# An attention kernel on one core: which engine's queue issues the two guard-row transfers of each unit

## The chip, the cores and the metric

The kernel runs on one core of a Trainium2 chip. Its time is the device time of one execution in microseconds, compared as the median of several runs. Lower is better.

## The reference, cut to what matters

The input x has 2048 rows of 128 numbers. The first block is full attention over all 2048 rows with 16 heads of 8 numbers and an additive bias; six further layers of windowed attention and feed-forward follow, which this change doesn't touch. The first block:

```
x = x + attn(layernorm(x))
q, k, v = (x @ Wq.T + bq), (x @ Wk.T + bk), (x @ Wv.T + bv)      # 16 heads of 8
logits = li[:, :, None, :] + lj[:, None, :, :] + rel_b           # 3 relations per (i, j)
relation_probs = softmax(logits, axis=-1)
bias = einsum('bijk,hk->bhij', relation_probs, logical_bias)
attn_scores = q·k / scale + gate * bias
out = softmax(attn_scores, axis=-1) @ v ;  out @ Wo.T + bo
```

## The kernel before, in words

The function `attention` computes the first block. The 2048 queries are 16 blocks of 128, and each block has two halves of 8 heads. One half of one block is a *unit*: there are 32 units, four to a `body` (`ul` 0 to 3), eight bodies (`it` 0 to 7). A unit has 16 *steps*, one for each block of 128 keys (`jb`), so the attention has 512 steps.

Each step makes two score tiles on TensorE. Tile **b** belongs to the present unit: query-key products (L529), then the relation bias (L537). ScalarE takes its exponential into `prob` (L660), and one step later TensorE multiplies `prob` with the values (L571). Tile **a** is the same product 24 steps ahead, and only its maximum over the keys is kept (L811, VectorE). The softmax needs that maximum. When a unit's 16 tiles a are through, VectorE and TensorE reduce them to one number for each head and query (events `max0`, `max1` after steps 8 and 10 of the unit before), split its negative into three bf16 parts, and transpose these (event `guard` after step 12; VectorE copies the result to `guardT` in step 13, L868). These 24 rows of 128 are the *guard rows*. Two small transfers, each 12 rows of 256 bytes, carry them from `guardT` into rows 48 to 50 of `qst` (L995). With them the product of tile b has 51 rows in place of 48, and so already subtracts the maximum. In step 0 of a unit TensorE first issues the query-key products of tile a, and then waits for `guard_dma` before those of tile b. There is no double buffer of `guardT`.

The relation bias comes from a second pipeline. Eight steps are a *window*: ScalarE, GpSimd and VectorE compute a quarter (512 keys) of the relation probabilities of a block in `stage`. SyncE sends it to DRAM (`quarter_out`, L973, waits for `lo_done`), waits until it has landed, and issues eight transfers of 128 KB back into `pst` in another layout (`quarter_in`, L986). Each unit has two windows and so two such bursts. The function `moved` issues one window's transfers.

The order on each engine is written out by hand: there is no scheduler. An engine's queue is in order, so whatever stands behind a wait waits too. SyncE's order in a unit is: at a block's start the queries of the next block (L963), `moved` for the even window, at a block's start the store of the finished block (L1026), `moved` for the odd window, `guards`.

In the last body no relation probabilities are left to compute after its first two windows, so `moved` issues nothing there after its first unit.

Of the kernel before, what the change touches and what calls it, by code (L numbers as in the profile page):

```python
# [27 lines left out]
NB = S // P  # L28
H, HD = 16, 8
HH = H // 2  # L30
# [3 lines left out]
GUARD_ROW = len(TERMS) * HD  # L34
# [354 lines left out]
def attention(nc, io, keep):  # L389

    with ExitStack() as ctx:
        sb = lambda n, s, d=F32: ctx.enter_context(nc.sbuf_tensor(n, s, d))
        sem = lambda n: ctx.enter_context(nc.semaphore(n))
        kst, qst, v9, coef = keep["kst"], keep["qst"], keep["v9"], keep["coef"]
# [32 lines left out]
        m_read = sem("m_read")  # L428
# [45 lines left out]
        def events_before(it, ul, step, first, last):  # L474

            n = 3 if first else 20 * it
            for w in range(ul + 1):
                e = unit_events(w, first, last)
                n = n + sum(1 for k in e if w < ul or k < step)
            return n  # L480
# [172 lines left out]
        @block.scalar  # L653
        def _(act):
            def exp_tile(b, st, first):
                act.wait_ge(b_done, b + 1)
                if not (first and st < 2):

                    act.wait_ge(pv_done, b - 1)
                act.activation(prob[:, st % 2, :], psS[:, slot_of("b", st)].rearrange("p a b -> p (a b)"), ACT.Exp)\  # L660
                   .then_inc(e_done, 1)

            def clamp(n, q, r, par):

                act.wait_ge(own_done, n // 4 + 1)
                if not (isinstance(n, int) and n < 2):
                    act.wait_ge(x_first, n - 1) if early(n - 2) else act.wait_ge(x_done, n - 1 - FIRST)
                    act.wait_ge(e2_done, n - 1)
                act.activation(top[:, r], f[:, 1, quarter(q)], ACT.Relu, bias=own[:, par, 1:2]).then_inc(u_done, 1)

            def third(n, r):

                act.wait_ge(top_done, n + 1)
                if not (isinstance(n, int) and n < 2):
                    act.wait_ge(pm_done, n - 1)
                act.activation(rec[:, r], top[:, r], ACT.Exp, scale=-1.0).then_inc(e2_done, 1)

            def pair_exp(n, r, par):

                act.wait_ge(x_first, n + 1) if early(n) else act.wait_ge(x_done, n + 1 - FIRST)  # L680
                act.activation(rel[:, r, 0], rel[:, r, 0], ACT.Exp, bias=own[:, par, 0:1])
                act.activation(rel[:, r, 1], rel[:, r, 1], ACT.Exp, bias=own[:, par, 1:2]).then_inc(re_done, 1)

            def first_part(n, r):

                act.wait_ge(pm_done, n + 1)
                if not (isinstance(n, int) and n < 2):
                    act.wait_ge(p_dma[r], n // 2 * (16 * PO))
                act.activation(stage[:, r, :, 0, :], rel[:, r], ACT.Copy).then_inc(hi_done, 1)

            def body(it, first=False, last=False):
                for st in range(4 * NB):
                    k, o, n, q, r, opens, closes = windows(it, st, last)
                    par = (k + EARLY) // 4 % 2
                    exp_tile(it * (4 * NB) + st, st, first)
                    if opens and o == 0:
                        clamp(n, q, r, par)
                    if closes and o == 2:
                        first_part(n - 1, 1 - r)
                    if opens and o == 2:  # L700
                        third(n, r)
                    if opens and o == 3:
                        pair_exp(n, r, par)

            for n in range(EARLY):
                clamp(n, n % 4, n % 2, n // 4)
                third(n, n % 2)
                pair_exp(n, n % 2, n // 4)
                if n >= 1:
                    first_part(n - 1, (n - 1) % 2)  # L710
            body(0, first=True)
            for it in range(1, 7):
                body(it)
            body(7, last=True)
# [241 lines left out]
        @block.sync  # L956
        def _(sp):
            def queries(block_no, par):
                t0 = block_no * P
                for hp in range(2):  # L960
                    src = io["q_stack"].rearrange("r (pair hp) s -> hp r pair s", hp=2)[hp]
                    src = src[:, :, t0:t0 + P] if isinstance(t0, int) else src[:, :, bass.ds(t0, P)]
                    sp.dma_start(qst[64 * hp:64 * hp + GUARD_ROW, par], src).then_inc(q_dma[par], 16)  # L963

            def quarter_out(n, q, r, blk, par):

                sp.wait_ge(lo_done, n + 1)
                take_waits(sp, sp_waits)
                if not (isinstance(blk, int) and blk < 2):
                    sp.wait_ge(pst_dma[par][q], blk // 2 * (16 * PI))  # L970
                take_waits(sp, sp_waits)
                there = p_parts[par, :, :, :, quarter(q)].rearrange("k a c j -> c (k a) j")
                sp.dma_start(there, stage[:, r].rearrange("p k a j -> p (k a) j")).then_inc(p_dma[r], 16)  # L973

            def quarter_in(n, q, r, blk, par):

                sp.wait_ge(p_dma[r], n // 2 * (16 * PO) + 16 * PO)
                take_waits(sp, sp_waits)
                if not (isinstance(blk, int) and blk < 2):
                    sp.wait_ge(b_done, (blk - 2) * (2 * NB) + NB + 4 * q + 4)  # L980
                take_waits(sp, sp_waits)
                for k in range(2):
                    for t in range(4):
                        w = 64 * k + G * t
                        there = p_parts[par, k, t // 3, :, quarter(q)].rearrange("(g i) j -> i g j", i=G)
                        sp.dma_start(pst[w:w + G, par, :, quarter(q)], there).then_inc(pst_dma[par][q], 16)  # L986

            def guards(read, ul):

                sp.wait_ge(m_read, read)  # L990
                par, half = (ul // 2) % 2, ul % 2
                for hp in range(2):
                    r = 64 * hp + GUARD_ROW
                    dst = qst[r:r + 3, par, HH // 2 * half:HH // 2 * (half + 1), :]
                    sp.dma_start(dst, guardT[12 * hp:12 * (hp + 1), :]).then_inc(guard_dma, 16)  # L995

            def moved(it, k, last):

                if not (last and k > 1):
                    n = it * 8 + k + EARLY - 1  # L1000
                    m = k + EARLY - 1
                    quarter_out(n, m % 4, m % 2, it * 2 + m // 4, m // 4 % 2)
                    quarter_in(n, m % 4, m % 2, it * 2 + m // 4, m // 4 % 2)

            def body(it, first=False, last=False):
                for ul in range(4):
                    blk = it * 2 + ul // 2
                    if ul % 2 == 0 and not (first and ul == 0) and not (last and ul == 2):

                        sp.wait_ge(b_done, blk * (2 * NB))  # L1010
                        take_waits(sp, sp_waits)
                        queries(blk + 1, (ul // 2 + 1) % 2)
                    moved(it, 2 * ul, last)
                    if ul % 2 == 0 and not (first and ul == 0):
                        store(blk - 1, events_before(it, ul, 6, first, last) + 1)
                    moved(it, 2 * ul + 1, last)
                    if not (last and ul == 3):
                        guards(events_before(it, ul, 12, first, last) + 1, (ul + 1) % 4)

            def store(blk, read):  # L1020

                sp.wait_ge(m_read, read)
                take_waits(sp, sp_waits)
                dst = io["x1"].rearrange("(b p) d -> p b d", p=P)
                dst = dst[:, blk, :] if isinstance(blk, int) else dst[:, bass.ds(blk, 1), :].rearrange("p a d -> p (a d)")
                sp.dma_start(dst, x1[:]).then_inc(x1_dma, 16)  # L1026

            queries(0, 0)
            queries(1, 1)
            for n in range(EARLY - 1):  # L1030
                quarter_out(n, n % 4, n % 2, n // 4, n // 4)
                quarter_in(n, n % 4, n % 2, n // 4, n // 4)
            guards(3, 0)
            body(0, first=True)
            for it in range(1, 7):
                body(it)
            body(7, last=True)
            store(NB - 1, 20 * 7 + 20 - 3 + 3)
            sp.wait_ge(x1_dma, 16 * NB)
# [747 lines left out]
```

## Time and profile before

| | |
|---|---|
| median of 3 runs | 3796.5 us (3795.06 to 3797.84) |
| the profiled execution | 3794.38 us, its span 3792.6 us |
| PE busy | 3167.1 us (84%) |
| DVE busy | 2489.9 us (66%) |
| ACT busy | 2070.3 us (55%) |
| POOL busy | 2294.9 us (61%) |
| DMA queue q1 (SyncE's) | 276232 packets, 252.24 MB, 31.3% of 16 engines' span |
| DMA queue q10 (ScalarE's) | 720 packets, 0.20 MB, 0.0% |

PE is TensorE, PEld its weight loads, DVE VectorE, ACT ScalarE, POOL GpSimd. SPq and ACTq rows are DMA issues of SyncE and ScalarE. An issue is not counted as busy time, and its row shows how long the issuing queue was taken, not how long the transfer took. "[5.32 <-DMA qst<-guardT]" behind a row says that the engine sat idle for 5.32 us before it, and that the transfer named ended this. The attention steps run from about 184 to 1604 us of the span; the first 184 us prepare, and the local layers fill the rest.

### The profile page before, as it was taken

To read this page: it belongs to the slowest core of one execution; us is meant where nothing else is said; L and a number is where in the kernel's file an instruction comes from. 1 tells how busy PE (TensorE), PEld (TensorE's weight loads), DVE (VectorE), ACT (ScalarE), POOL (GpSimd) and SP (SyncE) were. 2 spreads that over 40 slices of the span, in tenths; PEclk is the share of its full clock that TensorE was granted. 3 is DMA by queue.
4 is the path that set the end of the run, shared out by engine and by line. 5 is a ranking of instruction groups with operands and counts; after the bars stand their busy time and mean duration, and the time that the engine had idled before them with its cause. 6 is when DMAs were issued, how large, how long until landed. Compare 5 with 4: busy or idle time off the path is not lost. (4 is left out here: it accounts for less than half of the span.)

```text
span 3792.6 us, 121537 instructions
## 1 busy us (share of the span) xinstructions
PE 3167.1 (84%) x52983; PEld 2322.6 (61%) x52983; DVE 2489.9 (66%) x3404; ACT 2070.3 (55%) x2481; POOL 2294.9 (61%) x1606
## 2 busy tenths in 40 slices
PE   3488888888888888858888888888888888888885
PEld 2366666676666666636666666666666666666664
DVE  4766666766766666346666766766766667667663
ACT  2255445554544454426666666666666666666663
POOL 1544444444444443067777777777777777777773
PEclk7699999999999999979999999999999999999997
DMA  4544444444443443042223222322232232222221
GB/s 106 101 72 78 74 76 77 75 72 78 80 75 73 72 73 72 14 131 62 52 53 76 71 56 59 86 58 56 53 93 54 53 79 69 54 61 52 59 56 37
DMA packets 277483, 260.21 MB, mean 69 GB/s; under 512 B 106264, under 2 KB 220841, under 8 KB 276825
## 3 DMA queue, kind: packets, MB, share of 16 engines
q1 hardware_dynamic: 276232, 252.24, 31.3%
q8 instruction: 418, 6.85, 0.8%
q14 instruction: 113, 0.92, 0.1%
q10 hardware_dynamic: 720, 0.20, 0.0%
HBM read 98.30 MB, written 40.37 MB: 37 GB/s over the span
## 5 line engine op out<-in xcount | busy, mean ns | idle before, releaser
L660 ACT ACTIVATE prob<-psS 128x1024 f32<-128x1024 f32 x512 | 524.2, 1024 | 729.6 <-PE psS L537 726.2
L811 DVE TENSOR_TENSOR colmax<-psS,colmax 128x1024 f32<-128x1024 f32 x480 | 587.5, 1224 | 455.6 <-PE psS L537 453.4
L537 PE MATMUL psS<-diag,pst 128*128 128x64 bf16 x16384 | 609.6, 198 | 8.0 <-issue 7.8
L529 PE MATMUL psS<-qst,kst 48*128 48x128 bf16 (+1 forms) x8192 | 387.3, 225 | 250.1 <-DMA qst<-guardT 139.1
L537 PEld LDWEIGHTS psS<-diag,pst 128*128 128x128 f16 x16384 | 543.0, 101 | 69.0 <-issue 19.0
L1265 PE MATMUL R<-wqkv,xsT 128*128 128x512 f32 x1152 | 554.9, 605 | 1.5 <-ACT qT L1401 1.1
L745 POOL TENSOR_TENSOR rel<-rel,rec 128x1024 f32<-128x1024 f32 x64 | 151.9, 2373 | 626.6 <-DVE rec L824 626.6
L529 PEld LDWEIGHTS psS<-qst,kst 48*128 48x128 bf16 (+1 forms) x8192 | 242.0, 97 | 407.4 <-issue 163.0
L1529 POOL TENSOR_TENSOR pr<-pr,rnq 128x1024 f32<-128x1024 f32 x96 | 182.7, 1903 | 397.1 <-DVE pr L1610 397.1
L571 PE MATMUL psO<-prob,v 128*9 128x128 f32 x8192 | 333.1, 281 | 2.7 <-issue 2.1
L1265 PEld LDWEIGHTS R<-wqkv,xsT 128*128 128x128 f32 x1152 | 197.7, 191 | 162.2 <-issue 160.6
L1486 POOL TENSOR_TENSOR rnq<-ssq,half 128x16 f32<-128x16 f32 x96 | 281.6, 2934 | 8.0
L1486 POOL TENSOR_TENSOR rnk<-ssq,half 128x16 f32<-128x16 f32 x96 | 281.2, 2929 | 8.0
L1332 PE MATMUL R<-w,xnT 128*128 128x341 f32 x384 | 179.2, 601 | 100.7 <-DVE xnT L1594 100.7
L1499 POOL TENSOR_TENSOR t<-t 128x1024 f32<-128x1024 f32 x96 | 227.1, 2366 | 33.1 <-DVE t L1550 33.1
L1556 DVE TENSOR_REDUCE ssq<-sq 128x16 f32<-128x1024 f32 x192 | 233.2, 1214 | 11.2 <-ACT sq L1419 3.7
L1547 DVE TENSOR_TENSOR t<-R,tab 128x1024 f32<-128x1024 f32 x192 | 228.4, 1190 | 15.8 <-PE R L1265 9.3
L824 DVE RECIPROCAL rec<-tot 128x128 f32<-128x128 f32 x256 | 238.3, 937 | 0.0
L1603 DVE TENSOR_TENSOR gs<-hs 128x341 f32<-128x341 f32 x96 | 49.6, 516 | 285.9 <-ACT hs L1450 285.9
L1436 ACT ACTIVATE kT<-R 64x1024 f32<-64x1024 f32 x192 | 195.4, 1018 | 68.6 <-PE R L1316 67.4
L1520 POOL TENSOR_TENSOR t<-t 128x1024 f32<-128x1024 f32 x96 | 225.6, 2350 | 10.8 <-DVE t L1550 10.8
L1401 ACT ACTIVATE prT<-R 128x1024 f32<-128x1024 f32 x96 | 98.2, 1023 | 224.1 <-PE R L1286 224.1
(190 smaller groups left out, 6327.9 us busy)
## 6 DMA issues: line engine op xcount, KB each, us to landing
v<-vs SPq DMA_DIRECT2D x576, 128.0 KB, 2.4
pst<-p_parts SPq DMA_DIRECT2D x512, 128.0 KB, 4.9
p_parts<-stage SPq DMA_DIRECT2D x64, 512.0 KB, 3.1
v<-vs SPq DMA_DIRECT2D x384, 64.0 KB, 2.0
wqkv<-in_L_ffn_Wqkv SPq DMA_DIRECT2D x18, 512.0 KB
q_stack<-qpart SPq DMA_DIRECT2D x6, 512.0 KB
qst<-q_stack SPq DMA_DIRECT2D x32, 96.0 KB, 4.4
wo<-in_L_ffn_Wo SPq DMA_DIRECT2D x6, 512.0 KB
```

Source lines behind the costliest of these rows:

```text
L529: pe.matmul(dst[:, hp, P * p:P * (p + 1)], kst[r, pair, P * jb:P * (jb + 1)], qst[r, par, pair, :], start=(p == 0), stop=False, skip_group ...
L537: last = pe.matmul(o, pst[:, par, g, P * jb:P * (jb + 1)], diag[:, par, g, h0:h0 + HH // 2, :], start=False, stop=(g == NG - 1), skip_grou ...
L571: last = pe.matmul(psO[32 * c:32 * c + HD + 1, P * s:P * (s + 1)], v9[:, jb, HH * half + hl, :], prob[:, jb % 2, col:col + P], start=(jb = ...
L660: act.activation(prob[:, st % 2, :], psS[:, slot_of("b", st)].rearrange("p a b -> p (a b)"), ACT.Exp)\
L811: dve.tensor_tensor(dst, src, dst, ALU.max).then_inc(a_read, 1)
L824: dve.reciprocal(rec[:, r, cols], tot[:, r, cols]).then_inc(rr_done, 1)
L1265: last = pe.matmul(R[bank][:, c, :], xsT[:, par, :], w[:, INNER * which + 512 * c:INNER * which + 512 * (c + 1)], start=True, stop=True)
L1486: pool.tensor_tensor(dst, ssq[:, i, :], half1[:, 0:LH], ALU.pow).then_inc(m["rn_done"], 1)
L1499: pool.tensor_tensor(t1[:, 1, :], t1[:, 1, :], t2[:, 1, :], ALU.add).then_inc(m["add_done"], 1)
L1520: pool.tensor_tensor(t1[:, 0, :], t1[:, 0, :], t2[:, 0, :], ALU.add).then_inc(m["q_added"], 1)
L1547: dve.tensor_tensor(o1, q, tb(2 * i, 0, LD), ALU.mult)
L1556: dve.tensor_reduce(ssq[:, i, :], sq[:].rearrange("p (h d) -> p h d", d=LD), AX.X, ALU.add)\
```

## The change

ScalarE issues the guard transfers in place of SyncE. The function moves over unchanged but for the engine, and with its wait (`m_read`, that VectorE has written `guardT`). ScalarE calls it in step 13 of each unit but the last, directly behind the exponential of step 13, and once ahead of the first body.

```
@@ block.scalar
+            def guards(read, ul):
+                act.wait_ge(m_read, read)
+                par, half = (ul // 2) % 2, ul % 2
+                for hp in range(2):
+                    r = 64 * hp + GUARD_ROW
+                    dst = qst[r:r + 3, par, HH // 2 * half:HH // 2 * (half + 1), :]
+                    act.dma_start(dst, guardT[12 * hp:12 * (hp + 1), :]).then_inc(guard_dma, 16)
...
                     exp_tile(it * (4 * NB) + st, st, first)
+                    ul, jb = divmod(st, NB)
+                    if jb == 13 and not (last and ul == 3):
+                        guards(events_before(it, ul, 12, first, last) + 1, (ul + 1) % 4)
...
+            guards(3, 0)
             body(0, first=True)
@@ block.sync
-            def guards(read, ul):
-                sp.wait_ge(m_read, read)
...
                     moved(it, 2 * ul + 1, last)
-                    if not (last and ul == 3):
-                        guards(events_before(it, ul, 12, first, last) + 1, (ul + 1) % 4)
...
-            guards(3, 0)
             body(0, first=True)
```

SyncE's order over two units of the middle of the attention, before. L973 and L986 are `quarter_out` and `quarter_in`, L1026 stores a finished block, L963 loads the next block's queries:

```order
L1026 DMA x<-x_sb 128x128
L973 DMA p_parts<-stage 128x4x512
L986 DMA pst<-p_parts 16x8x512 x8
L995 DMA qst<-guardT 3x4x128 x2
L973 DMA p_parts<-stage 128x4x512
L986 DMA pst<-p_parts 16x8x512 x8
L973 DMA p_parts<-stage 128x4x512
L986 DMA pst<-p_parts 16x8x512 x8
L995 DMA qst<-guardT 3x4x128 x2
L963 DMA qst<-q_stack 48x8x128 x2
```

The same place of SyncE after the change (L986 and L999 are now `quarter_out` and `quarter_in`, L1028 the store, L976 the queries):

```order
L1028 DMA x<-x_sb 128x128
L986 DMA p_parts<-stage 128x4x512
L999 DMA pst<-p_parts 16x8x512 x8
L986 DMA p_parts<-stage 128x4x512
L999 DMA pst<-p_parts 16x8x512 x8
L986 DMA p_parts<-stage 128x4x512
L999 DMA pst<-p_parts 16x8x512 x8
L976 DMA qst<-q_stack 48x8x128 x2
```

The guard transfers stood behind the eight `pst` transfers of the odd window; they are gone from this queue, and nothing else changed its place.

ScalarE's order over the second half of a unit and the start of the next, before. L660 is the exponential of a step; the others belong to the relation windows:

```order
L681 ACTIVATE rel<-rel,own 128x512
L682 ACTIVATE rel<-rel,own 128x512
L660 ACTIVATE prob<-psS 128x1024 x5
L669 ACTIVATE top<-f,own 128x512
L660 ACTIVATE prob<-psS 128x1024 x2
```

And after:

```order
L681 ACTIVATE rel<-rel,own 128x512
L682 ACTIVATE rel<-rel,own 128x512
L660 ACTIVATE prob<-psS 128x1024 x2
L698 DMA qst<-guardT 3x4x128 x2
L660 ACTIVATE prob<-psS 128x1024 x3
L669 ACTIVATE top<-f,own 128x512
L660 ACTIVATE prob<-psS 128x1024 x2
```

The two issues stand between the exponentials of steps 13 and 14; those of steps 14, 15 and of step 0 of the next unit are queued behind them.

## Rows read from the trace of the kernel before

**Rows 1.** The page: one of the costliest groups, busy time, then idle time ahead
```profile
L529 PE MATMUL psS<-qst,kst 48*128 48x128 bf16 (+1 forms) x8192 | 387.3, 225 | 250.1 <-DMA qst<-guardT 139.1
```

**Rows 2.** TensorE's waits, 200 to 1600: who for whom, us, times, longest
```profile
PE psS L529 <- DMA qst<-guardT: 134.0, 29, 6.1
PE psS L537 <- issue: 7.8, 10, 1.4
PE psS L529 <- issue: 4.1, 6, 1.1
PE psO L571 <- issue: 2.1, 3, 0.8
```

**Rows 3.** Timeline, steps 13 of a unit to 1 of the next: start, length
```profile
856.37 1.03 ACT L660 ACTIVATE prob<-psS 128x1024 f32<-128x1024 f32 x1 [1.95 <-PE psS L537]
856.78 5.10 SPq L986 DMA_DIRECT2D pst<-p_parts  x8
857.04 0.27 DVE L868 CAST guardT<-psM 24x128 bf16<-24x128 f32 x1
858.66 1.02 ACT L660 ACTIVATE prob<-psS 128x1024 f32<-128x1024 f32 x1 [1.26 <-PE psS L537]
859.81 1.11 PE L537 MATMUL psS<-diag,pst 128*128 128x64 bf16 x32
860.84 0.62 PE L571 MATMUL psO<-prob,v 128*9 128x128 f32 x16
861.40 0.40 PE L529 MATMUL psS<-qst,kst 48*128 48x128 bf16 x8
861.93 1.55 SPq L995 DMA_DIRECT2D qst<-guardT  x2
867.12 0.60 PE L529 MATMUL psS<-qst,kst 51*128 51x128 bf16 x8 [5.32 <-DMA qst<-guardT]
867.65 1.89 PE L537 MATMUL psS<-diag,pst 128*128 128x64 bf16 x32
870.38 0.62 PE L529 MATMUL psS<-qst,kst 48*128 48x128 bf16 x16
```

**Rows 4.** Windows: busy us of each engine, PEclk, DMA share, GB/s
```profile
864.00:865.00 1.00, 0.00 (x0) 0.00 (x0) 0.00 (x0) 0.00 (x0) 0.00 (x0) 1.00 1.14 122
866.00:867.00 1.00, 0.00 (x0) 0.00 (x0) 0.00 (x0) 0.00 (x0) 0.00 (x0) 0.92 0.05 8
867.00:869.00 2.00, 1.88 (x34) 1.69 (x35) 0.27 (x1) 0.00 (x0) 0.00 (x0) 0.50 0.03 8
1508.00:1604.00 96.00, 93.08 (x2483) 70.62 (x2478) 37.00 (x56) 48.42 (x48) 0.00 (x0) 1.00 0.02 4
```

**Rows 5.** Timeline of the last body, one unit's end, where no `pst` burst runs
```profile
1539.96 0.27 DVE L868 CAST guardT<-psM 24x128 bf16<-24x128 f32 x1
1540.26 1.44 SPq L995 DMA_DIRECT2D qst<-guardT  x2
1544.32 0.85 PE L529 MATMUL psS<-qst,kst 48*128 48x128 bf16 x16
1546.70 0.76 PE L529 MATMUL psS<-qst,kst 48*128 48x128 bf16 x16
```

**Rows 6.** ScalarE's timeline: step 0 of units 0, 29 and 30
```profile
184.48 1.02 ACT L660 ACTIVATE prob<-psS 128x1024 f32<-128x1024 f32 x1 [25.69 <-PE psS L537]
1507.28 1.02 ACT L660 ACTIVATE prob<-psS 128x1024 f32<-128x1024 f32 x1 [7.44 <-PE psS L537]
1546.25 1.02 ACT L660 ACTIVATE prob<-psS 128x1024 f32<-128x1024 f32 x1 [1.36 <-PE psS L537]
```

**Rows 7.** DMA issues by line: ns min/median/max; ScalarE's own at the start
```profile
L995 SPq DMA_DIRECT2D qst<-guardT x64: 698/736/806, 179.3 to 1573.6; - x64
L231 ACTq DMA_DIRECT2D bk<-in_L_attn_bk x1: 453/453/453, 2.6 to 2.6; - x1
```

**Rows 8.** TensorE's timeline beside an even window's burst
```profile
388.45 1.08 PE L537 MATMUL psS<-diag,pst 128*128 128x64 bf16 x31 [1.36 <-issue]
```

More of the change, by code:

```diff
@@ L986, in quarter_in @@
                         sp.dma_start(pst[w:w + G, par, :, quarter(q)], there).then_inc(pst_dma[par][q], 16)
-            def guards(read, ul):
-                sp.wait_ge(m_read, read)
[L991 to L995, printed above, removed]
             def moved(it, k, last):
```

## The prediction

> **What bounds the kernel now.** I read the page first. In the attention part TensorE is busy in nearly every slice, and the group of the query-key products is the one group of TensorE with much idle time: 250.1 us, of which 139.1 us ended with the arrival of `qst<-guardT` [rows 1]. The list of waits, cut to the attention's steps, says how that is spread: 29 times, 134.0 us, 6.1 us the longest [rows 2], so 4.62 us each. The thirtieth wait of the page, ahead of the first unit, makes up the other 5.1 us. No other wait of TensorE there reaches 16 us in sum. So TensorE sets the pace of the attention, and once in each unit it stands still for the guard rows.
>
> The timeline says why [rows 3]. VectorE has the guard rows ready at 857.31 us (857.04 + 0.27). SyncE is then already issuing the eight `pst` transfers of the odd window, from 856.78 for 5.10 us, and gets to the guard rows at 861.93, 4.6 us after they were ready. TensorE had issued tile a's products of step 0 at 861.40 and wanted tile b's at 861.80. It gets them at 867.12. Of that time the guard transfers spend about 3.5 us behind the burst: the 16 DMA engines are still full at 864 to 865 (share 1.14), and empty at 866 to 867 (0.05) [rows 4].
>
> The pause has a second price. After it the granted clock is 0.50, the 1.2 GHz level, at 867 to 869, where TensorE worked throughout [rows 4]; the relation products of that step take 1.89 us and not 1.11 [rows 3]. From the products of tile a in step 0 to those of step 1 it takes 870.38 - 861.40 = 8.98 us, where the same distance without a wait is 1546.70 - 1544.32 = 2.38 us [rows 3, 5]. The difference, 6.60 us, is 5.32 us of idle time and 1.28 us of slow clock.
>
> The trace contains the changed order too, as far as SyncE can show it. In the last body the odd window of units 29 and 30 has no burst, so nothing stands in front of the guard issue. In unit 29 the rows are ready at 1540.23, are issued at 1540.26, and TensorE goes through all 16 products of step 0 at 1544.32 with no wait [rows 5]. The lead is 1544.72 - 1540.26 = 4.46 us, and it was enough on idle DMA engines.
>
> **The change part by part.** *The wait goes.* Two ways to size it:
> - From the parts: 134.0 us of idle time [rows 2], and 29 times 1.28 us of slow clock = 37 us. Together 171 us. It is a lower end: in some units the slow clock lasts longer than in the one shown.
> - From whole units: units 0 to 28 take (1507.28 - 184.48) / 29 = 45.61 us each, and unit 29, whose end has no wait, 1546.25 - 1507.28 = 38.97 us [rows 6]. The difference, 6.64 us, times 29 is 193 us. It is an upper end: unit 29 also lacks the instruction stalls below, and as a block's second unit the two small products of a finished block.
>
> I take the middle, 182 us. The clock's part goes with the pause: from 1508 to 1604, with two unit ends without a wait, the granted clock is 1.00 over the whole 96 us with TensorE busy for 93.08 [rows 4].
>
> *What ScalarE takes on.* Two issues in each of 31 units, and two ahead of the first. On SyncE the same issue takes 0.736 us, on ScalarE the only ones there are took 0.453 us [rows 7], so 0.9 to 1.5 us for the pair. ScalarE ends the exponential of step 13 at 857.40, and the one of step 14 starts at 858.66: a gap of 1.26 us [rows 3]. The wait on `m_read` costs nothing, since the rows are ready at 857.31, before that exponential ends. With the longer pair (857.40 to 858.9) the exponential of step 14 ends at 859.9 instead of 859.68. The first who needs it is TensorE's value product at 860.84 [rows 3]. Slack 0.9 us, price 0. The bound on the other side: if an issue takes more than about 1.2 us on ScalarE, the excess, twice, reaches TensorE. Steps 14 and 15 have only their exponential, so ScalarE is back in time by step 15.
>
> *SyncE.* It loses two issues in each unit and a wait. Behind them stand the queries of the next block, which wait for the unit's end anyway, and the next window, 17 us later. Gain and loss 0. The burst itself stays where it is.
>
> *When the guard rows land now.* The first issue starts at about 857.4, the second at 858.1. They are needed at 861.80: the lead is 4.4 us, the same as in unit 29 (4.46 us), but now a burst runs beside them. Bounds: no wait at all, as in unit 29; or the time that the transfers took in the row of before, 867.12 - 861.93 = 5.19 us, then with some 3.5 us of burst in front of them. That gives 857.4 + 5.2 = 862.6, a wait of 0.8 us, 23 us over 29 units. At 858.1 only some three of the eight `pst` transfers have been issued, so I am nearer to the first: 0.2 us, 6 us in all. I don't expect so short a pause to bring the slow clock back; the 1.36 us of rows 8 didn't (its 31 products take 1.08 us, full speed).
>
> *What is late next.* TensorE's instructions come over the same DMA engines. Beside a burst of an even window it stops in the middle of a product group: 1.36 us before 388.45, ended by "issue" [rows 8]. All such stops together are 7.8 + 4.1 + 2.1 = 14.0 us [rows 2], about 0.5 us in a unit, and they lie some 5.5 to 9 us after the issue of an even burst. The same stretch of the odd burst (862 to 866) is now covered by the wait for the guard rows. With that wait gone I expect the same there: 14 us, between 0 and 29 us (1 us in each). The other candidate is `pst`: the last quarter of a block, issued from 856.78, is needed four steps after the unit's end, at about 861.8 + 4 x 2.3 = 871. The burst is through by 866, so 0, with 4 us to spare.
>
> *Sum.* 182 - 14 - 6 = 162 us. The profiled execution took 3794.4 us, so 3632 us; the median of the runs is 2.1 us above it, so **3634 us**.
>
> The Trainium skill (page "DMA: Bandwidth & Descriptors", section "Issuing engines are not separate DMA queues") says that transfers of all issuing engines run on the same 16 DMA engines, and that a second issuing engine only saves the issuing time, usually small. By that rule alone, the gain would be the 4.6 us of issue time and nothing of the queueing. In this trace issuing is what is late, and the two can't be parted: an earlier issue is also ahead of most of the burst.
>
> **The rivals.**
> - *The burst still holds them up in part.* The guard transfers start early but are served or completed only in the middle of the burst, about 864.5. TensorE idles 2.7 us, half of now. For it: the DMA engines are at a share above 1 for some seven microseconds, and one `pst` transfer of 128 KB needs nearly one of them. Against: few are ahead at 858. Gain 29 x 2.7 = 78 us, up to 115 us if the clock stays up: 3680 to 3720 us.
> - *Their completion is held until the burst is through.* The issue moves, the landing doesn't: TensorE resumes at 867 as before, ScalarE's delay hides in the pause, and the time is 3796 us, within 0.2%. For it: in before the release came about 1 us after the engines had run empty, so completion isn't instant beside large writes. Against: most of the burst is issued after the guard rows. The Trainium skill ("DMA: Bandwidth & Descriptors", section "Queues, rings and completion order") says that the write that raises the semaphore lands only after every earlier write of that DMA engine, across its queues. That would hold the guard rows behind the writes already under way, not behind those issued later; no row here shows it apart from the queueing.
> - *Slower: ScalarE is held at its issue.* If the two issues don't go through while SyncE feeds its burst, ScalarE stands from 857.4 until the burst has drained, about 865.5, and pays its 1.5 us then. The exponential of step 14 ends at 868.1; then follow the value product (0.56), tile a's products (0.40) and tile b's at about 869.2 instead of 867.1: 2.1 us more in each of 29 units, 61 us, 3857 us. It decides from a hold of some 8 us; with less the present wait covers it. Against: issues on ScalarE took 0.45 us at the start, and the longest on SyncE for the same transfer 0.806 us [rows 7].
> - *TensorE would stop there anyway*, for instructions. Priced above at 14 us; if it were 2 us in each unit, 58 us, the time would be 3678 us. It is within the range.
>
> **How the numbers follow.** The forecast 0.76: its own range is from 193 us gained (3603) to 171 - 29 - 23 = 119 us (3677). The partly held transfers 0.12, the held completion 0.07, ScalarE held 0.05 with any other loss. What a measurement of this kernel can tell from no change is 0.2%, 7.6 us. Faster 0.88, same 0.07, slower 0.05. The range, 3605 to 3700, leaves out the last two cases, half of the first rival and a small rest at the lower end: 0.19.
>
> **What would show it.** The wait `L529 <- DMA qst<-guardT` of 134.0 us should be under 25 us. ScalarE's queue should show the two issues between the exponentials of steps 13 and 14, at 0.45 to 0.75 us each, and the exponential of step 14 late by under 0.4 us, without TensorE waiting at L571. The dips of the granted clock, one in each unit, should be gone, and a unit should take about 39.5 to 40 us and not 45.6. TensorE's "issue" stops should rise from 14 to some 28 us. The local layers should take the same time as before. I am wrong if TensorE still waits over 1 us for the guard rows, if it waits at L571 for `prob`, or if `pst` becomes a wait.

## The result, and the profile after

| | before | after |
|---|---|---|
| median of four runs each | 3795.8 us (one run more than above) | 3664.7 us (3660.3 to 3667.6) |
| ratio, 95% interval | 1 | 0.9656 (0.9639 to 0.9672) |
| the profiled execution, its span | 3794.4, 3792.6 us | 3663.7, 3661.9 us |

The profiled execution gained 130.7 us. The forecast was 162 us and 3634 us, so the time lies in the range, 31 us above the forecast value.

TensorE's waits in the attention, 183 to 1500 us of the changed kernel, in the columns of [rows 2] (who for whom: us, times, longest):

```profile
PE psS L529 <- DMA qst<-guardT: 29.0, 22, 3.0
PE psS L537 <- issue: 13.7, 18, 2.7
PE psO L571 <- issue: 5.4, 10, 1.0
PE psS L529 <- issue: 5.1, 7, 1.5
```

The guard wait fell from 134.0 us to 29.0 us, and did not vanish. The stops that end in "issue" rose from 14.0 us to 24.2 us.

Two unit ends of the changed kernel, to be laid beside [rows 3]. First one without a wait:

```profile
871.54 5.34 SPq L999 DMA_DIRECT2D pst<-p_parts  x8
872.11 1.02 ACT L660 ACTIVATE prob<-psS 128x1024 f32<-128x1024 f32 x1 [1.94 <-PE psS L537]
872.78 0.27 DVE L881 CAST guardT<-psM 24x128 bf16<-24x128 f32 x1
873.08 1.49 ACTq L698 DMA_DIRECT2D qst<-guardT  x2
874.68 1.02 ACT L660 ACTIVATE prob<-psS 128x1024 f32<-128x1024 f32 x1 [1.55 <-PE psS L537]
877.14 0.86 PE L529 MATMUL psS<-qst,kst 48*128 48x128 bf16 x16
```

Then one with it:

```profile
1323.34 4.10 SPq L999 DMA_DIRECT2D pst<-p_parts  x8
1324.61 1.54 ACTq L698 DMA_DIRECT2D qst<-guardT  x2
1326.25 1.02 ACT L660 ACTIVATE prob<-psS 128x1024 f32<-128x1024 f32 x1 [1.59 <-PE psS L537]
1329.02 0.40 PE L529 MATMUL psS<-qst,kst 48*128 48x128 bf16 x8 [0.30 <-DVE colmax L824]
1330.66 0.40 PE L529 MATMUL psS<-qst,kst 51*128 51x128 bf16 x8 [1.23 <-DMA qst<-guardT]
```

ScalarE issues 0.03 us after VectorE has written `guardT` (873.05, 873.08), without a wait of its own. The pair takes it 1.5 us, and the exponential of step 14 starts 0.3 us late. The lead is 4.5 us in the first (to 877.5) and 4.8 us in the second (to 1329.4). In the first it was enough. In the second TensorE went on 6.05 us after the issue, later than the 5.19 us of [rows 3], which I had taken for the end of the range. The trace's records of single DMA packets say where the time went: the first packet of the guard rows starts 1.42 us after the issue in the first unit and 2.83 us in the second. Where no burst runs, in the last body, it is 1.37 us.

The 1.23 us of idle time don't cost speed: the eight products behind it take 0.40 us. A longer wait can. At the end of unit 0 the idle time is 1.93 us, and behind it the clock is lower and the relation products take 1.89 us again; at another unit's end they take 1.11 us behind 2.49 us of idle time. TensorE's timeline at both, and the window behind the first (columns as in [rows 4]):

```profile
220.20 0.50 PE L529 MATMUL psS<-qst,kst 51*128 51x128 bf16 x8 [1.93 <-DMA qst<-guardT]
220.63 1.89 PE L537 MATMUL psS<-diag,pst 128*128 128x64 bf16 x32
```
```profile
754.13 0.40 PE L529 MATMUL psS<-qst,kst 51*128 51x128 bf16 x8 [2.49 <-DMA qst<-guardT]
754.46 1.11 PE L537 MATMUL psS<-diag,pst 128*128 128x64 bf16 x32
```
```profile
222.00:224.00 2.00, 2.00 (x42) 1.39 (x39) 2.00 (x3) 1.44 (x2) 0.13 (x1) 0.55 0.01 4
```

Over units 0 to 28 the mean granted clock rose from 0.94 to 0.99. The windows of these units, of the kernel before and of the changed one:

```profile
184.48:1507.28 1322.80, 1160.02 (x30043) 904.24 (x30045) 894.15 (x1124) 663.45 (x750) 593.09 (x315) 0.94 0.43 75
```
```profile
180.41:1376.33 1195.92, 1127.25 (x30043) 873.98 (x30045) 907.68 (x1124) 663.51 (x750) 592.45 (x315) 0.99 0.48 83
```

Both hold the same 30043 products of TensorE. They took 1160.0 us before and 1127.3 us after, so 32.8 us of slow clock were won.

ScalarE's exponentials at step 0 of units 0 and 29, as in [rows 6]:

```profile
180.41 1.02 ACT L660 ACTIVATE prob<-psS 128x1024 f32<-128x1024 f32 x1 [26.07 <-PE psS L537]
1376.33 1.02 ACT L660 ACTIVATE prob<-psS 128x1024 f32<-128x1024 f32 x1 [5.19 <-PE psS L537]
```

A unit takes (1376.33 - 180.41) / 29 = 41.24 us, where it took 45.61 us. The 29 units gave 126.9 us. That is 105.0 us less wait for the guard rows and 32.8 us less slow clock, less 10.2 us more of "issue" stops; the parts meet it to 1 us. Another 4.1 us were gained ahead of unit 0. They are scatter and not the change: TensorE's wait for the guard rows there is 5.6 us and was 5.1 us, its waits for `pst` happened to be 3.8 us shorter, and in the eleven traces of this document step 0 of unit 0 starts anywhere from 179.0 to 186.9 us. The local layers did not change: TensorE is busy 1840.3 us in the last 2187 us of the span, and was 1841.2 us in the last 2188 us.

### The profile page after: what moved, and what is told of

Read it like the earlier page. It is cut to its first block and busy times, and to the rows that moved or that the text cites. A ratio compares the mean times of both kernels' runs of the same rounds, so it can differ in the third digit from the quotient of the medians.

```text
span 3661.9 us, 121537 instructions
## 1 busy us (share of the span) xinstructions
PE 3133.4 (86%) x52983; PEld 2292.0 (63%) x52983; DVE 2503.8 (68%) x3404; ACT 2070.3 (57%) x2481; POOL 2294.0 (63%) x1606
## 5 line engine op out<-in xcount | busy, mean ns | idle before, releaser
L660 ACT ACTIVATE prob<-psS 128x1024 f32<-128x1024 f32 x512 | 524.2, 1024 | 603.0 <-PE psS L537 599.9
L537 PE MATMUL psS<-diag,pst 128*128 128x64 bf16 x16384 | 587.3, 195 | 13.9 <-issue 13.7
L537 PEld LDWEIGHTS psS<-diag,pst 128*128 128x128 f16 x16384 | 520.9, 99 | 74.1 <-issue 20.5
L571 PE MATMUL psO<-prob,v 128*9 128x128 f32 x8192 | 326.3, 276 | 6.0 <-issue 5.4
L1500 POOL TENSOR_TENSOR t<-t 128x1024 f32<-128x1024 f32 x96 | 227.1, 2366 | 35.4 <-DVE t L1551 35.4
L1548 DVE TENSOR_TENSOR t<-R,tab 128x1024 f32<-128x1024 f32 x192 | 228.5, 1190 | 18.1 <-PE R L1266 9.3
```

The costliest lines, as they stand in the source:

```text
L537: last = pe.matmul(o, pst[:, par, g, P * jb:P * (jb + 1)], diag[:, par, g, h0:h0 + HH // 2, :], start=False, stop=(g == NG - 1), skip_grou ...
L571: last = pe.matmul(psO[32 * c:32 * c + HD + 1, P * s:P * (s + 1)], v9[:, jb, HH * half + hl, :], prob[:, jb % 2, col:col + P], start=(jb = ...
L1500: pool.tensor_tensor(t1[:, 1, :], t1[:, 1, :], t2[:, 1, :], ALU.add).then_inc(m["add_done"], 1)
L1548: dve.tensor_tensor(o1, q, tb(2 * i, 0, LD), ALU.mult)
```

## The experiments

All were timed against the kernel before on the same chip; times are medians. Theory A: what is left of the wait is the guard rows' packets sharing the DMA engines with the burst. Theory B: ScalarE's own queue lands them late.

**1. The guard rows from SyncE, ahead of the burst.**

```
@@ kernel before, SyncE
                     quarter_out(n, m % 4, m % 2, it * 2 + m // 4, m // 4 % 2)
+                if between:            # guards(...) in the odd windows
+                    between()
                     quarter_in(n, m % 4, m % 2, it * 2 + m // 4, m // 4 % 2)
```

> SyncE issues the guard rows again, but between quarter_out and quarter_in of the odd window, so ahead of the burst in the same queue. Theory A (the 29.0 us that TensorE still waits after the change are the guard rows' packets sharing the DMA engines with a burst that started 0.5 us earlier): ahead of the burst they land about 2.2 us after their issue, as in the last body, TensorE waits under 3 us in all, the slow clock goes too, about 3625 to 3640 us. Theory B (the wait is a longer landing on ScalarE's own queue): the same, so this run alone does not part A and B, but after_small does. Rival: the burst now starts some 2 us later and nearer to its use, and the instruction stops or a wait for pst take back what is won: 3650 to 3670 us.

Measured: 3661.8 us, ratio 0.9656 (0.9638 to 0.9675), the same as the changed kernel. The guard wait is gone; no row for it is left. In its place stand the instruction stops (183 to 1500):

```profile
PE psS L537 <- issue: 28.6, 25, 2.9
PE psS L529 <- issue: 14.5, 11, 2.4
PE psO L571 <- issue: 10.1, 14, 1.6
```

They add up to 53.2 us, where the changed kernel has 24.2 us. One of them, at the start of a unit, with the queue of SyncE ahead of it:

```profile
873.92 1.56 SPq L995 DMA_DIRECT2D qst<-guardT  x2
875.66 3.64 SPq L986 DMA_DIRECT2D pst<-p_parts  x8
```
```profile
882.09 0.62 PE L571 MATMUL psO<-prob,v 128*9 128x128 f32 x16
885.13 1.03 PE L529 MATMUL psS<-qst,kst 48*128 48x128 bf16 x16 [2.42 <-issue]
```
```profile
880.00:882.00 2.00, 2.00 (x64) 1.54 (x56) 2.00 (x4) 1.54 (x2) 0.39 (x1) 1.00 1.17 133
882.00:884.00 2.00, 0.71 (x22) 0.38 (x18) 2.00 (x2) 1.02 (x1) 1.97 (x1) 1.00 1.06 124
```

TensorE stops while the DMA share is above 1, and goes on when the burst is through. So the rival's mechanism was right: what is won on one wait comes back in the other. Sorted by the burst in front of them, 35.1 us of these stops lie behind odd bursts and 18.1 us behind even ones; in the changed kernel it is 5.4 and 19.1 us. The odd ones stand where the 29.0 us of guard wait stood, so this wait was largely a cover for them. That the burst also starts some 2 us later here was not tested apart.

**2 and 3. The odd windows' burst cut to an eighth of its bytes**, in the kernel before and in the changed one, from body 1 on. Seven of eight groups of `pst` keep old values in those windows.

```
-                        sp.dma_start(pst[w:w + G, par, :, quarter(q)], there)...
+                        ng = 1 if small else NG      # small: it > 0 and k odd
+                        sp.dma_start(pst[w:w + G, par, 0:ng, quarter(q)], there[:, 0:ng])...
```

> Kernel before, with the eight pst transfers of the odd windows from body 1 on cut to an eighth of their bytes (one of eight groups; the rest of pst keeps old values, so that part of the result is left out). SyncE still issues all eight ahead of the guard rows. It parts issue time from queueing. If the 5.3 us wait is issue time of SyncE alone, it stays near 5 us in each unit and the time at 3785 to 3796 us. If it is issue time and queueing, the guard rows land 2.2 us after an issue at the old moment: wait 2 to 2.5 us, 60 to 75 us in all, 3690 to 3720 us. If it is queueing alone, no wait: 3625 us.

> Changed kernel with the same cut of the odd windows' burst (part of the result left out). Theory A: no wait for the guard rows from body 1 on (under 6 us in all, from body 0), the instruction stops fall from 24 us to about 14 (those of the even windows): 3610 to 3630 us. Theory B (ScalarE's queue lands them late by itself): the wait stays at 25 to 30 us, 3650 to 3665 us.

Measured: before with the cut 3675.8 us, ratio 0.9692 (0.9676 to 0.9708). Changed kernel with the cut 3621.4 us, ratio 0.9549 (0.9530 to 0.9567). TensorE's guard waits, first of before with the cut, then of the changed kernel with the cut:

```profile
PE psS L529 <- DMA qst<-guardT: 52.2, 27, 4.7
```
```profile
PE psS L529 <- DMA qst<-guardT: 2.3, 3, 1.6
```

SyncE still issues the eight transfers ahead of the guard rows, and the wait falls all the same. Of the 52.2 us, 16.8 us belong to the four units of body 0, where the burst is not cut. The other 25 units have 35.4 us, 1.4 us each in place of 4.6 us. So the wait of before was part issue time (some 1.4 us) and part queueing behind the burst (some 3.2 us, which includes what SyncE saves on the smaller issues). The 2.3 us of the changed kernel with the cut lie all in body 0. My expectation of 3690 to 3720 us was too high: SyncE was also through its eight smaller issues sooner (4.40 us in the unit that I looked at, against 5.10), and most of the slow clock went with the first 3 us (mean 0.98 over 200 to 1400). The Trainium skill ("DMA: Bandwidth & Descriptors", section "Issuing engines are not separate DMA queues") says that issuing from several engines saves only the issuing time. No run here speaks against it. In the units shown the issue moved 4.6 us ahead, and a unit became 4.4 us shorter, and experiment 1 reaches the same time without a second engine. The place in the queue changed less: the first packet of the guard rows starts on average 3.4 us after their issue in the kernel before, 2.3 us in the changed one and 1.4 us where nothing is in front of it.

Theory B falls: with the burst cut, ScalarE's queue delivers in time. The "issue" stops fell to 10.3 + 5.4 + 3.6 = 19.3 us, not to the expected 14 us: the stops behind even bursts are 18.2 us here and were 14.0 us in the kernel before. Why they grew stays open.

**4. Two more issues on ScalarE** in step 13, behind the guard rows.

```
+                for hp in range(2):
+                    act.dma_start(extra[12 * hp:12 * (hp + 1), :], extra_src[...]).then_inc(extra_dma, 16)
```

> Changed kernel with two more issues on ScalarE behind the guard rows in step 13, of the same shape, to a buffer that nobody reads. Theory (slack of 0.9 us ahead of TensorE's value product, so the change's own issues cost nothing): the exponential of step 14 is late by 0.3 + 1.5 = 1.8 us, 0.9 us of it reach TensorE as a wait of L571 for prob, partly taken back from the guard wait: 10 to 26 us more than the changed kernel, 3675 to 3690 us. Rival (the change's own two issues already cost TensorE time): the two more cost their full 1.46 us in each of 29 units, 42 us, 3705 us or more. Rival (ScalarE's issues hide wholly): no change, 3665 us.

Measured: 3670.6 us, ratio 0.9679 (0.9663 to 0.9695), 6 us above the changed kernel by the medians, below the 3675 to 3690 us that I expected; the two intervals overlap. The waits (183 to 1500; L575 is the value product) show why that is so little:

```profile
PE psO L575 <- ACT prob L664: 29.4, 32, 1.7
PE psS L533 <- DMA qst<-guardT: 8.8, 10, 1.8
```

TensorE now waits 0.9 us for the exponential of step 14 in each of 32 places, as expected. That wait lies ahead of the guard wait, and takes 20 us of it over. The change's own two issues cost TensorE next to nothing: its profile has a single wait of 0.6 us at L571 for `prob`.

**5. The guard rows issued one step later.**

```
-                    if jb == 13 and not (last and ul == 3):
+                    if jb == 14 and not (last and ul == 3):
```

> Changed kernel with the two issues behind the exponential of step 14 instead of 13, 2.3 us later. Theory: the landing moves with the issue and the lead falls from 4.4 to about 2.1 us, so TensorE waits about 2 us more in each unit, 29 + 60 = 90 us in all, and the slow clock comes back in part: 3725 to 3745 us. Rival (the landing is set by the end of the burst and not by the issue): the wait grows little, 3665 to 3680 us.

Measured: 3736.6 us, ratio 0.9863 (0.9838 to 0.9888). Against the changed kernel that is 72 us by the medians and 78 us by the ratios, since the two ran on different chips. The guard wait, 183 to 1500:

```profile
PE psS L529 <- DMA qst<-guardT: 90.8, 29, 4.3
```

62 us more wait for 2.3 us less lead in 29 units (67 us): the landing moves with the issue.

**6 and 7. The burst paced by TensorE's steps**, with the guard rows on ScalarE and with those of experiment 1 on SyncE.

```
+                        if pace:                       # ahead of each of the eight
+                            sp.wait_ge(b_done, pace[4 * k + t])
...
+                    step = it * (4 * NB) + 8 * k + 4
+                    pace = [step + (i // 2 if k % 4 == 1 else i) for i in range(8)]
```

> Changed kernel, and the eight pst transfers of a window are no longer issued at once: SyncE waits for b_done ahead of each, so one goes out in each step (two in each step in the windows whose quarter is needed soonest). Same transfers, same bytes, same instructions of TensorE. Theory C (beside a burst that fills the DMA engines both the guard rows and TensorE's instruction reads come late; only what is in front of them at that moment counts): the guard wait falls from 29 us to under 8, the instruction stops from 24 us to under 10, 3605 to 3630 us. Rival (the stops are not tied to the burst): the stops stay at 24 us, 3630 to 3640 us. Rival (paced transfers reach pst too late and TensorE waits for pst): above 3665 us.

> SyncE issues the guard rows ahead of the odd window's pst transfers (as sp_first), with the same pacing. Theory C: no guard wait, and the 53 us of instruction stops of sp_first fall to under 15: 3605 to 3630 us, the same as act_spread, so ScalarE is not needed for the gain. Rival (the stops of sp_first come from SyncE's queue and not from the density of the burst): they stay near 50 us, 3655 to 3665 us.

Measured: on ScalarE 3623.2 us, ratio 0.9567 (0.9549 to 0.9585); on SyncE 3628.2 us, ratio 0.9580 (0.9561 to 0.9599). TensorE's waits for the guard rows and for "issue" (183 to 1434) with the guard rows on ScalarE, then on SyncE:

```profile
PE psS L529 <- DMA qst<-guardT: 15.4, 13, 2.7
PE psS L529 <- issue: 2.5, 1, 2.5
PE psO L571 <- issue: 2.2, 2, 1.3
PE psS L537 <- issue: 0.4, 1, 0.4
```
```profile
PE psS L537 <- issue: 10.0, 9, 2.5
PE psS L529 <- issue: 7.3, 5, 2.7
PE psO L571 <- issue: 5.2, 4, 2.9
```

The stops fall from 24.2 to 5.1 us, and from 53.2 to 22.5 us, with the same bytes and the same instructions of TensorE. The rival that they are not tied to the burst falls. The guard wait fell to 15.4 us, not below the 8 us that I expected, and on SyncE the stops stayed above 15 us. Both sit nearly on the same total, as experiment 1 and the changed kernel do without the pacing. So which engine issues the guard rows matters little once they are issued in step 13.

**8 and 9. A wider pace where the quarter is needed soonest**, beside a repeat of experiment 6 on the same chip.

```
-                    pace = [step + (i // 2 if k % 4 == 1 else i) for i in range(8)]
+                    pace = [step + (i * 5 // 7 if k % 4 == 1 else i) for i in range(8)]
```

> As act_spread, but in the windows whose quarter is needed soonest the eight pst transfers go out over six steps and not four (the last one in step 17, needed from step 20). In act_spread the guard wait and the stops that are left lie almost only at the ends of those units. Theory C (what is left is the density of these windows' transfers): 5 to 15 us less than act_spread, guard wait under 8 us, 3610 to 3618 us. Rival (the last quarter now comes too late): a wait for pst at step 20, 3630 us or more. Rival (what is left is not tied to density): within 5 us of act_spread.

> act_spread once more, unchanged, on the same chip as act_spread5, for the comparison of the two: 3620 to 3630 us by every theory.

Measured: 3624.5 us, ratio 0.9544 (0.9524 to 0.9564), and for the repeat 3627.4 us, ratio 0.9555 (0.9535 to 0.9575): no difference that the runs can tell, and not the 5 to 15 us that theory C gave. The guard wait, first with the wider pace, then in the repeat:

```profile
PE psS L529 <- DMA qst<-guardT: 21.4, 15, 4.7
```
```profile
PE psS L529 <- DMA qst<-guardT: 22.9, 15, 5.6
```

The repeat is the kernel of experiment 6, whose trace had 15.4 us. One trace of this wait is thus good to some 8 us only, and a rest of 15 to 23 us is not shown to be a matter of this pace.

## Why the prediction held, point by point

- **What bounds, and why the wait was there.** Right. The guard rows were late because SyncE was issuing the burst, and because they then queued behind it. Experiment 2 parts the two, and experiment 5 shows that the landing moves with the issue.
- **The wait goes: 182 us.** Too large by some 15 us, before any rest of the wait is counted. It is 134 us of wait and 48 us beside it. The slow clock gave 32.8 us, close to the 37 us of the first way; few slow products are left (in units 0 to 28 the relation products of some eight steps, before of about forty). The upper end of 193 us had the instruction stops and a block's small products in it, as the prediction says itself, and taking the middle counted part of them as clock.
- **ScalarE's two issues: 0.** Right, by the waits for `prob`; experiment 4 fits. An issue took 0.73 us, near the long end.
- **When the guard rows land: 0.2 us of wait in a unit, 6 us.** This is the step that was mis-sized most. It is 29.0 us, 1.0 us on average and over 1 us in 12 of the 29 units, where the prediction's own sign was under 25 us. I had taken the 5.19 us of one unit of before as the worst landing beside a burst. Landings of 6 us occur also from an issue only 1.3 us behind the burst's first, so a single row was no bound. The rival of the partly held transfers was true in part. Experiment 3 shows the cause: without the burst the wait is 0 from body 1 on.
- **What is late next: instruction stops, 28 us.** 24.2 us. The kind is right, the size in part luck. I expected 14 us more, all behind odd bursts; there are 5.4 us behind those and 5.0 us more behind even ones. The place was read wrong too: the stops of before start 7.3 to 10.5 us after the first issue of their burst (8.5 us in [rows 8]), not 5.5 to 9 us. Experiment 1 shows that the odd ones were sheltered: with the guard rows quite out of the way they are 35 us, beyond the 29 us that I had set as the most.
- **The sum.** 23 us more of guard wait and 15 us less won from the clock, against 4 us less of stops and 4 us of scatter ahead of unit 0: 30 of the 31 us between 162 and 131 us. A unit takes 41.24 us and not the 39.5 to 40 us of the prediction.
- **SyncE and the local layers: 0; `pst` not late.** Right.
- **The slower rival.** ScalarE was not held at its issue: the pair took 1.49 to 1.54 us in the 29 units, while SyncE fed its burst.

## What to carry to other kernels

A small transfer that an engine will wait for should be issued in the moment its data is ready, from a queue in which no bulk transfer stands ahead; here that gave 3.4%. Then look at how the bulk transfers themselves are spread: here a burst that kept the DMA share above 1 for some 7 us delayed the guard rows and went with TensorE's stops, and pacing it with one wait ahead of each transfer gave another 1% (0.9567 of before). When one wait is taken away, ask what it covered in the same microseconds.

## What the runs showed of the hardware that was not expected

```profile
q8 instruction: 418, 6.85, 0.9%
```

- The same two transfers of 12 x 256 bytes, issued at the same point of a unit with the same burst beside them, were in time after 4.5 us in one unit and took 6.05 us in another, 7.42 us at the longest. Over the 29 units their first packet starts 1.37 to 4.50 us after the issue; in the seven units without a wait it is at most 1.53 us. The wait goes with how fast SyncE issued the burst: in the seven units where that took 4.2 us or less the wait was 1.2 to 3.0 us, 14.7 us of the 29.0 us in all; of the eleven where it took 5.19 us or more, seven had none. Which of the two causes the other, or whether a third thing causes both, stays open.
- With a pause of 5 us in each unit the granted clock averaged 0.94, with one of 1 us 0.99. Single pauses do not sort as simply: behind one of 1.93 us the products were slow, behind one of 2.49 us they were not.
